# A four-layer decoder: the first batch's sum, norm and turning made inside eight attentions, and the leads' projections in rows

## The reference, cut to what matters

```python
x = _layernorm(x + attn(x)); x = _layernorm(x + xattn(x, ctx)); x = _layernorm(x + ffn(x))   # four times
# eight softmax attentions of 16 heads among them; one of them:
scores = jnp.einsum('bnhr,bmhr->bhnm', Qr, Kr) / math.sqrt(RANK)
A = jax.nn.softmax(scores, axis=-1)
out = jnp.einsum('bhnm,bmhv->bnhv', A, V).reshape(b, n, d)
return out @ WO + bO
```

## Time and profile before

| | us |
|---|---|
| median of 3 runs | 1648.59 |
| lowest and highest | 1648.35, 1649.25 |
| the profiled execution's own time | 1639.49 |
| span of its trace | 1637.7 |
| PE busy in the span | 1444.5 (88%) |
| PE weight loads busy | 681.8 (42%) |
| DVE busy | 1047.1 (64%) |
| ACT busy | 667.2 (41%) |
| POOL busy | 218.8 (13%) |

### The profile page before, as it was taken

How to read it: one execution, slowest core, us unless ns; L and a number is a source line. 1 busy time by engine, 2 the same in 40 slices (tenths; PEclk the granted TensorE clock), 3 DMA queues, 4 the chain that set the end, 5 groups by cost and what they waited for, 6 DMA issues and landing times. The chain is left out here.

```text
span 1637.7 us, 22279 instructions
## 1 busy us (share of the span) xinstructions
PE 1444.5 (88%) x8409; PEld 681.8 (42%) x8409; DVE 1047.1 (64%) x2625; ACT 667.2 (41%) x952; POOL 218.8 (13%) x235
## 2 busy tenths in 40 slices
PE   2899789996778889999899999899998879999886
PEld 2232344443553434445444333446444633335344
DVE  6696665457985677774555696365755666774555
ACT  3466453223326013333453466443323345544533
POOL 3000000001000434443100000000000012332002
PEclk9799799997879889999999899999999889999999
DMA  5000000003000010000002000000001000000000
GB/s 225 1 1 1 1 1 1 0 0 151 1 0 2 1 52 1 2 1 1 1 1 108 6 1 1 1 1 1 1 0 77 0 1 1 1 1 1 1 1 13
DMA packets 4105, 27.15 MB, mean 17 GB/s; under 512 B 416, under 2 KB 2464, under 8 KB 2976
## 3 DMA queue, kind: packets, MB, share of 16 engines
q1 hardware_dynamic: 4000, 25.74, 4.0%
HBM read 25.21 MB, written 0.52 MB: 16 GB/s over the span
## 5 line engine op out<-in xcount | busy, mean ns | idle before, releaser
L955 DVE TENSOR_REDUCE maxima<-banks 128x1 f32<-128x512 f32 (+4 forms) x640 | 363.1, 603 | 110.7 <-PE banks L802 104.1
L1120 ACT ACTIVATE big<-banks 128x1024 f32<-128x1024 f32 (+2 forms) x320 | 294.4, 960 | 268.7 <-PE banks L845 93.9
L830 PE MATMUL banks<-big 32*128 32x512 f32 (+6 forms) x1280 | 234.8, 621 | 17.2 <-DVE big L976 12.9
L802 PE MATMUL banks<-big 32*128 32x77 bf16 (+6 forms) x1024 | 156.0, 293 | 19.1 <-DVE negmaxT L978 4.5
L868 PE MATMUL banks<-big,v_heads 128*9 128x512 f32 (+7 forms) x1024 | 160.5, 573 | 6.3 <-ACT heads_out L1015 3.2
L1737 DVE TENSOR_TENSOR big<-big,banks 128x512 f32<-128x512 f32 (+1 forms) x116 | 79.7, 687 | 113.5 <-PE banks L1588 91.2
L802 PEld LDWEIGHTS banks<-big 32*128 32x128 bf16 (+1 forms) x1024 | 55.8, 95 | 179.5 <-DVE maxima L955 95.0
L1713 ACT ACTIVATE big<-banks 128x512 f32<-128x512 f32 (+1 forms) x116 | 69.0, 595 | 145.1 <-PE banks L1587 144.9
L1618 PE MATMUL banks<-big,moe_weights 128*128 128x512 f32 (+1 forms) x232 | 119.9, 601 | 3.4 <-DVE big L1746 3.4
L613 POOL TENSOR_TENSOR rstd<-mean_var,minus_half 128x4 f32<-128x4 f32 x34 | 35.3, 1038 | 591.4 <-DVE mean_var L530 591.4
L830 PEld LDWEIGHTS banks<-big 32*128 32x128 f32 (+3 forms) x1280 | 73.4, 179 | 70.3 <-ACT big L1120 23.5
(11 more groups left out here) (429 smaller groups left out, 2144.2 us busy)
## 6 DMA issues: line engine op xcount, KB each, us to landing
moe_weights<-in_moe SPq DMA_DIRECT2D x1, 4864.0 KB, 14.6
moe_weights<-in_moe SPq DMA_DIRECT2D x1, 4768.0 KB, 23.3
moe_weights<-in_moe SPq DMA_DIRECT2D x1, 3264.0 KB, 10.6
moe_weights<-in_l3x SPq DMA_DIRECT2D x1, 3072.0 KB, 10.4
late_weights<-in_l2x SPq DMA_DIRECT2D x1, 2048.0 KB, 7.9
moe_weights<-in_l SPq DMA_DIRECT2D x1, 1234.0 KB, 13.2
rows<-in_rows SPq DMA_DIRECT2D x1, 1152.0 KB, 8.1
late_weights<-in_turned SPq DMA_DIRECT2D x1, 1152.0 KB, 17.5
```

What stands on the lines that cost most here:

```text
L802: last = nc.tensor.matmul(RING[n % NR][:, x * klen:x * klen + last_key(t)], q[rows, t * P:(t + 1) * P], ks[rows, 0:last_key(t)], start=Tru ...
L830: last = nc.tensor.matmul(SC[pair % 2][0:size, j % 2, n0:S], ks[rows, i * P:i * P + size], q[rows, n0:S], start=True, stop=turned)
L955: nc.vector.tensor_reduce(dst, src, AX_X, ALU.max).then_inc(ring_free.up(), 1)
L1120: nc.scalar.activation(E[pair % NEP][0:size, :, n0:S], SC[pair % 2][0:size, :, n0:S], ACT.Exp, scale=scale).then_inc(exp_ready.up(), 1)
```

## The change

It has four parts.

**1. Half 0's end becomes items of the ring.** `go_inside()` marks a deferred `Norms` as begun. Batch 0's front turning, sum and turning are three further items, filled at rounds `at_front`, `at_sum` and `at_turn` between batch 1's groups, and VectorE empties each at its place: the front's copy, the residual add with the statistics, the norm a round or two later, and the scaled move of the turned half. The power is GpSimd's, between its own work of two rounds where it has any. Nothing of half 0 is left in the tail or in the next block. For the attention with 77 keys and head size 8 (16 heads, 8 rounds) and for a2, `first_written + 1` is round 7 or 8, so that all or nearly all of it falls into the tail; for the others it lies in the middle of batch 1.

```diff
+    def go_inside(self):
+        self.inside = self.begun = True
+        self.FRONT, self.SUM, self.TURNED = (None, 6), (None, 6), (None, None, 6, None)
+        return self
...
+    first_written = NG // B * nkt - 1 + (turn_after if turned else later)
+    at_front = first_written + 1
+    at_sum = at_front + (1 if finish and finish.front else 0)
+    at_norm = at_sum + (2 if nkt > 1 else 1)
+    at_turn = at_norm + 1
...
+    def first_half_filled(pe, r):
+        if r == at_front and finish.front:
+            if not finish.front.make:
+                heads_done(pe, 0)
+            bank = fill_item(pe, "front")
+            finish.turn_front(pe, 0, bank[:, 0:S // 2].bitcast(BF16) if finish.front.bf else bank, ring_ready)
+        if r == at_sum:
+            if finish.front:
+                pe.wait_ge(ring_free.sem, ring_free.at(norm_item["front"] + 1))
+            else:
+                heads_done(pe, 0)
+            for _ in finish.add_up(pe, 0, fill_item(pe, "sum"), ring_ready):
+                pass
+        if r == at_turn:
+            finish.turn_half(pe, 0, fill_item(pe, "turned"), ring_ready)
...
+    def first_half_emptied(dve, r):
+        if r == first_written:
+            finish.take_row(dve)
+            if finish.front and finish.front.make:
+                heads_done(dve, 0)
+                finish.front.make(dve, finish.step, 0).then_inc(finish.front_made.up(), 1)
...
+        if r == at_sum:
+            finish.own_sum(dve, 0, empty_item(dve), ring_free)
+            finish.own_stats(dve, 0, 0)
+        if r == at_norm:
+            finish.own_norm(dve, 0, 0)
+        if r == at_turn:
+            bank = empty_item(dve)
+            for dst, g, b in finish.final.turned:
+                last = copy_scaled(c, nc.vector, dst[:, 0:S], bank[:, :], g, b)
+            last.then_inc(ring_free.up(), 1)
...
-                if r == R or r == R + 1 and added_up or r > R and summed(r - turn_after) is not None:
+                if defer:
+                    first_half_filled(pe, r)
+                elif r == R or r == R + 1 and added_up or r > R and summed(r - turn_after) is not None:
                     next(product, None)
```

```diff
             prior.front_second(pe)
-            product = prior.product_second(pe)
-            if prior.front:
-                for _ in product:
-                    pass
-                for _ in range(5):
-                    nc.tensor.matmul(c.bank[5][:, :], c.ident_bf[:], c.pick.rearrange("p j m -> p (j m)"), start=True, stop=True)
-            else:
-                for _ in range(ST - 1):
-                    next(product)
-            prior.turn_half(pe, 0)
-            for _ in product:
-                pass
             for s in range(N + LAG + 1):
+                if s == 1:
+                    for _ in prior.product_second(pe):
+                        pass
...
-            prior.first_half(dve)
             norm = prior.second_half(dve)
```

```diff
-                upto = min(max(wanted, made + (first > 0)), len(projections))
+                paced = max(early, dense) + int(first // 2 * pace) if first < lead else made + 1
+                upto = min(max(wanted, made, paced), len(projections))
```

145 lines of the change are left out of this document (98 added, 47 removed).

## The result

The changed kernel takes 1664.42 us in the median (1663.02 to 1665.45, 4 runs), the kernel before 1648.92 beside it (1648.35 to 1651.46): a ratio of 1.009, 95% interval 1.0073 to 1.0108. That is 15.5 us slower, where +8.2 was forecast; the upper end of the range was 1665.

A forecast was written before the change was run, and what follows sets the result against it. Attentions were taken as running at full clock with 3 to 6% of TensorE time free in middle rounds; handovers, tails, rounds and leads summed to +8.2 us, 1656.8 us on the median, range 1641 to 1665.

The forecast's parts named there:

- Rival A: Attention rounds have room: half of the 29.9 us inside costs is absorbed, -6.8 us in all, to 1641.8; chance 0.24.
- The absorption: Batch 1's rounds: free engine time takes up part of the added work, about 2 us in layer 0's attention, less elsewhere.
- -3.7 in the two with head size 64: Tails of layer 1's causal and layer 2's cross attention: half of the 7.5 us of sum pieces saved, -3.7 us each.
- a2's +5.1: a2's tail: sum in one row and waiting for half 0's turning end the block about 5.1 us later.
- the +3 in the tail of layer 0's cross attention: Layer 0's cross attention: all items fall into the tail, whose chain ends three us later.
- a1's feed-forward block, -2.3: Feed-forward block after a1: first product starts without half 0's turning, -2.3 us, sized from a2's block.
- The MoEs: MoEs of layers 1 and 2: `up(0)` starts without the earlier products, gaining 1.1 and 1.7 us.
- rival C: Tails of causal and layer 2's cross attention: clock falls, sum and `up` behind them slow, +13 to 1662; chance 0.17.
- The cross lead of layer 2: Handover from layer 2's attention: 2.3 + 1.11 us ahead of half 1 and half a us of turning go, -3.9.
- The leads: Projections in rows in layer 1's cross attention, -1.3 us, and reordered lead in layer 2's attention, -2.0 us.
- layer 1's cross attention's -1.3: Lead of layer 1's cross attention: projections in a dense row bring 2.4 GHz sooner, -1.3 us, bounds 0 and -2.
- The -2.0 for layer 2's own lead: Lead of layer 2's attention: queries and keys replace value projections ahead of the first turning, -2.0 us, bounds -4 and +3.

The follow-up runs named there:

- four-item form: Kernel before with all new leads and layer 1's causal attention inside, half 0's sum split into four items of 16 records: 1636.59 us, ratio 0.9946.
- the leads alone: Kernel before with only the change's new order of the leads, all seven deferred ends as before: 1632.48 us, ratio 0.9911.
- experiment 4: Kernel before plus seven products that nobody reads in the tail of layer 2's attention: 1650.37 us, ratio 1.0009.
- experiment 5: Kernel before with the new order of leads in the cross attentions of layers 0, 1 and 2 only: 1636.93 us, ratio 0.9924.
- experiments 2 and 3: Here, 2: changed kernel with the old leads' order, 1689.70 us; 3: changed kernel plus seven unread products in layer 2's attention's tail, 1668.66 us.

## Why the prediction was right in sign and half in size

**The direction and the mechanism.** The forecast was that the rounds lose more than the handovers and tails give back, and so it is. Rival A (the rounds have room) is refuted by the causal attention's +9.6 and its four-item form; with it goes the reading of the weight loads that I had taken from the Trainium skill ("Perfetto Trace Analysis", section "Identifying the Most-Contended Engine"), which speaks of how near TensorE is to its limit: weight loads were busy for 43% of the time there, and still nothing was absorbed. For what a round absorbs, the busy share of TensorE was the better guide here.

**The absorption, the term that was mis-sized in every attention.** I took 29.9 us for the rounds, after absorbing 2, 1.7, 0.8, 0.4 and 0.3 of the added 35.1. Measured: +9.8 in layer 0's attention (forecast 6.5), +4.7 in layer 2's against the leads alone (4.3), +9.6 (7.3), +8.8 (7.7), and in a1 +5.2 between two traces without half clock in its rounds, 131.8 against the 126.5 of experiment 4 (4.1). Together 38, more than the 35 us of work that I had counted before absorption. Up to 3 of the 9.8 can be half clock (0.93 over those rounds, 0.95 before); the other four had the same clock on both sides. So the absorption that I had put at 5.2 us was none. In layer 0's attention I had also counted VectorE's items alone; TensorE's busy time in the rounds grew too, by 5.0 us (94.04 to 99.02, some of it by the clock), for its front, sum and turning. Idle time of one engine in such a round is time in which the other works for it; it isn't free.

**The tails and the short attentions.** -3.7 in the two with head size 64 was -3.66 and -3.60; a1's -1.5 was -1.7; a2's +5.1 was +4.7, its feed-forward -2.3 was -2.2; the +3 in the tail of layer 0's cross attention was +3.25 against before, 4.5 against the leads alone. These were sized from single rows and chains, and stood. One that I had carried over from a2 didn't: a1's feed-forward block, -2.3, gave only 0.6 (26.8 to 26.2), at a mean clock of 0.94 where it had been 1.00.

**The MoEs.** I gave them -1.1 and -1.7; they lost 0.7 and 1.1. The step that failed is that `up(0)` first is worth anything: it only moves the 7.5 us of the sum behind it, where both VectorE (8.23 us idle) and ScalarE (7.72) wait for the second expert, and part of the sum ran at half clock (8.48 us for 64 records that took 7.38 in the rounds). That 1.1 us is what came of rival C there, and without it layer 1's MoE would be about even.

**The cross lead of layer 2.** -3.9 forecast, +4.2 between the traces. The chain is shorter as I said: with the clock kept it took 25.45 us, against 28.74, -3.3. But the clock fell (0.74). With the front and sum gone from the tail before it, seven products there kept the clock up in two kernels of two, so the emptier tail has its part in it; it isn't the whole cause, since experiment 4's trace, with front and sum in that tail, has 0.76 and 35.72 us. Against that trace, which is like the usual executions, the lead is 2.8 us *shorter*. I had the clock as a rival, at other places (rival C: the two tails that lost products, and the MoE behind them); it came at the first products behind layer 2's attention. The Trainium skill's picture of bursts that begin cold after a wait ("TensorE: Matmul & The Clock Gate", section "HAM oscillation — how this bites in real kernels") fits only in part: the records behind the waits took 1.85 us instead of 1.16, but the waits were of 0.7 to 0.9 us, the clock was still 1.00 behind them, and it fell within a row of products. In the tails that I had named the clock stayed.

**The leads.** I took -3.3; alone they give -16.3. The sum was made on a profiled execution that was 9 us faster than the median, a difference that I carried along as a constant. By the trace of experiment 4 it is half clock in the very leads that the change reorders, and the trace that I read couldn't show it. So the leads had more to give than the trace held, and what they gave may be nearly all clock (up to 14 of 15.1 us by the estimate there). Of the two terms that I had, layer 1's cross attention's -1.3 was -1.1 after and -2.1 with the leads alone. The -2.0 for layer 2's own lead isn't there: lead and rounds together took 129.9 us before and 130.5 with the leads alone. Layer 0's own lead, for which I had no term, was 1.4 to 3.1 us shorter, but as short with its old order (18.2 us, experiment 5).

**The two errors pull against each other.** Leads 13 us better than forecast, items some 20 us worse: 31.9 us is what the seven cost on top of the new leads, where I had 11.5. About 20 of that is in the terms named: 8.1 in the rounds, 4.6 in the two MoEs, 5.5 in layer 2's cross lead (+1.6 against the leads alone for -3.9), 1.7 in a1's feed-forward block. The forecast of +8.2 against +15.5 is closer than its terms, and that the result still lies below 1665 is luck: each of the two errors alone is larger than the 8.2 us from the forecast's 1656.8 to that bound.

**What stays open.** How the granted clock is decided from one handover to the next: the same instructions of layer 2's cross lead ran at 0.84 in the leads alone and at 1.00 with one earlier attention changed. In the whole change the filled lead's gain of 7.5 us was lost at other places, and with one attention inside it was kept. I can show where the clock was low, not why it moved.

## What to carry to other kernels

Don't fill a loop's idle shares before asking who waits for whom: where two engines alternate, a short wait on the one is work on the other, and added instructions cost their full length (here 38 us for 35, up to 3 of it clock). Take a change apart before judging it: this one held a part worth -16 us, by the estimate nearly all of it clock, and a part worth +41 (or +32 beside the first), and the first part alone was 32 us faster than both. And where a profiled execution is faster than the median, compare the mean granted clock of the executions and find the stage that differs before using it as the base of a sum; here it lay in the stages that the change touched.

## What the runs showed of the hardware

Whether a handover runs at 2.4 or at 1.2 GHz can change without a change in its own instructions: the same lead took 26.8 or 31.4 us with one code, and 25.45 or 32.95 with another, by whether seven idle-filling products of up to 0.25 us stood in the tail ahead. The executions of the kernel before spread from 1638 to 1653 us, with mean granted clocks from 0.948 down to 0.938: two profiles caught the lower end, and that of a near copy the upper one, with 0.76 instead of 1.00 as the clock of one lead. And two kernels that differ ahead of a point (experiments 2 and 3) ran the 500 us behind it alike to 0.05 us in every stage.
